# Weights of the sampling step laid out with four output rows side by side

## The reference

```python
samp = (v00 * (1 - wx) + v01 * wx) * (1 - wy) + (v10 * (1 - wx) + v11 * wx) * wy
return jnp.einsum('hwpc,hwp->hwc', samp, m)
```

## Time and profile before

| | |
|---|---|
| median of 3 runs | 6316.8 us (6306.65 to 6329.6) |
| profiled execution | 6298.82 us, span of the instructions 6297.0 us |
| VectorE (DVE) busy | 5355.5 us, 85% |
| TensorE (PE) busy | 3268.4 us, 52%, mean granted clock 0.763 |
| ScalarE (ACT) busy | 1498.1 us, 24% |
| GpSimd (POOL) busy | 529.3 us, 8% |
| DMA | 473.40 MB, 75 GB/s, 24.1% of 16 engines on SP's queue |

### The profile page before, as it was taken

One profiled execution on the slowest core, in us unless ns is written; L12 is line 12 of the kernel. 1 busy time (PEld: TensorE's weight loads), 2 busy tenths in 40 slices (PEclk: granted clock), 3 DMA queues, 4 the chain that ended last, 5 costly groups with the idle time before them and its releaser, 6 DMA issues.

```text
span 6297.0 us, 42119 instructions
## 1 busy us (share of the span) xinstructions
PE 3268.4 (52%) x15026; PEld 1887.4 (30%) x15026; DVE 5355.5 (85%) x6273; ACT 1498.1 (24%) x1409; POOL 529.3 (8%) x293
## 2 busy tenths in 40 slices
PE   4442645655455465645656455465645646455345
PEld 2211323332232233223333233233323333232233
DVE  5689898888989889898898989889898888989861
ACT  1312212222132223222222231223222222231210
POOL 0000101001010010001001010010001001010000
PEclk8676777878778687877878777687877878778677
DMA  7102122231222213122231222213122121222243
GB/s 322 50 17 64 56 73 68 60 95 40 77 87 61 77 53 102 41 75 68 60 95 50 76 78 67 71 53 102 41 75 75 57 91 50 70 83 62 70 110 87
DMA packets 511491, 473.40 MB, mean 75 GB/s; under 512 B 367984, under 2 KB 449904, under 8 KB 507568
## 3 DMA queue, kind: packets, MB, share of 16 engines
q1 hardware_dynamic: 507296, 463.25, 24.1%
q0 software_dynamic: 3984, 7.45, 0.5%
HBM read 229.00 MB, written 241.57 MB: 75 GB/s over the span
## 4 chain that ended last, share of the span: by engine, by line
DVE 68%; PE 16%; ACT 6%; issue 6%; POOL 3%; DMA 1%; SPq 1%; DVEq 0%; POOLq 0%; ACTq 0%
DVE spread L1102 9%; DVE partial L1092 9%; DVE spread L1092 6%; DVE qx L764 5%; DVE work L764 5%; PE ps L475 5%; DVE work L826 4%; DVE work L817 4%; DVE partial L1109 3%; PE ps L586 3%; PE ps L645 3%; DVE partial L1108 3%; DVE stats L735 2%; PE ps L656 2%; POOL small L1355 2%
## 5 line engine op out<-in xcount | busy, mean ns | idle before, releaser
L1102 DVE TENSOR_TENSOR spread<-spread,partial 128x1344 f32<-128x1344 f32 x384 | 685.4, 1785 | 13.3
L645 PE MATMUL ps<-band,near 128*16 128x128 f32 (+1 forms) x8192 | 655.3, 489 | 79.5 <-DMA near<-img_dram 79.5
L1092 DVE TENSOR_TENSOR partial<-haty,hatx 128x1344 f32<-128x1344 f32 x384 | 679.4, 1769 | 5.5
L543 PE MATMUL ps<-work,w2x 128*128 128x512 f32 x1152 | 558.0, 614 | 161.7 <-DVE work L817 150.7
L1224 ACT ACTIVATE xp<-x,small 128x1024 f32<-128x1024 f32 x128 | 280.2, 2332 | 1401.8 <-POOL small L1355 1401.8
L645 PEld LDWEIGHTS ps<-band,near 128*16 128x16 f32 x8192 | 486.5, 127 | 294.5 <-issue 103.4
L1092 DVE TENSOR_TENSOR spread<-haty,hatx 128x1344 f32<-128x1344 f32 x288 | 458.0, 1590 | 85.7 <-ACT qx L1261 64.4
L475 PE MATMUL ps<-qx,work 128*128 128x512 f32 x512 | 277.8, 704 | 333.4 <-DVE work L843 332.7
L656 PE MATMUL ps<-samp,wout 128*128 128x256 f32 x1024 | 296.7, 441 | 283.6 <-ACT samp L1330 260.8
L817 DVE SCALAR_TENSOR_TENSOR work<-ps,cols,qx 128x512 f32<-128x512 f32 x576 | 403.2, 746 | 14.3 <-PE ps L543 5.5
L586 PE MATMUL ps<-wts,work 128*128 128x432 f32 x512 | 223.0, 601 | 369.1 <-ACT work L1305 369.1
(11 more groups left out here) (229 smaller groups left out, 5262.5 us busy)
## 6 DMA issues: line engine op xcount, KB each, us to landing
band<-taps_dram SPq DMA_DIRECT2D x512, 288.0 KB
taps_dram<-partial SPq DMA_DIRECT2D x832, 72.0 KB, 2.1
near<-img_dram SPq DMA_DIRECT2D x256, 128.0 KB
img_dram<-band SPq DMA_DIRECT2D x6, 4096.0 KB, 40.9
om_now<-om SPq DMA_DIRECT2D x32, 576.0 KB, 5.2
om_dram<-om SPq DMA_DIRECT2D x32, 576.0 KB, 6.0
taps_dram<-partial SPq DMA_DIRECT2D x320, 54.0 KB, 2.1
x<-x_in SPq DMA_DIRECT2D x16, 1024.0 KB, 10.4
```

What stands on the lines that cost most here:

```text
L543: pe.matmul(bank(4 + i % 4), w2x[:, half, tap, :], tr[:, h * HALF:(h + 1) * HALF], start=True, stop=True).then_inc(s_w, 1)
L645: mm = pe.matmul(o, near[:, j, g * CG:(g + 1) * CG], band[:, :, a:z, j * G + g], start=False, stop=(j == JB - 1), skip_group_check=True)
L1092: return build(vec.tensor_tensor(o, haty[:, :, 3 * i:3 * i + 3, :].rearrange("p e j a -> p j e a"), cells, ALU.mult))
L1102: done = build(vec.tensor_tensor(skew, skew, spare, ALU.add))
```

## The change

Four output rows lie side by side in the band: its free axes become (block of four rows, column block, column slot, group, row in block). One block of four rows reaches 12 image rows, 96 partitions. The moving operand of a sampling matmul is then 2 blocks x 12 or 16 columns x 4 rows with the four rows adjacent in memory, 16 bytes. The matmuls keep their number and shapes.

What follows from it: the points of an image are put in another order, so that the partitions of a tile are 8 row blocks x 16 columns and the tile number holds the row in the block. The Gelu writes that order, in four instructions an image instead of two. A row of weights in the ring has 12 reached rows x 64 (zeros where a row doesn't reach), and lines 1108 and 1109 write it skewed, with a step of four numbers. SP writes a slot in eight DMAs instead of four. The band is loaded in 8 DMAs of 96 partitions. The copy to `samp` reads PSUM in the new order. Here `YB` is 8, `REACHED` 12, `QB` 2 and `YI` 4. The weights in DRAM are 26.7 MB instead of 18.9 MB (both are zeroed at the start), the rows that GpSimd gathers lie in the work tile, and the home pixel of a far tap takes one more instruction.

```diff
-        taps_dram = dram("taps_dram", [2, H, D * BW, SLOTS * HG])
+        taps_dram = dram("taps_dram", [2, YB, REACHED, ROW])
-        band = sb("band", [P, QROWS, SLOTS, HG])
+        band = sb("band", [P, QB, JB, SLOTS, G, YI])
-        gat = sb("gat", [P, 2, PAIR])
+        gat = work[:, 4 * N - 2 * PAIR:4 * N].rearrange("p (y c) -> p y c", y=2)
...
-                for yl in range(QROWS):
-                    sp.dma_start(band[yl * BW:yl * BW + D * BW, yl, :, :].rearrange("p s h -> p (s h)"),
-                                 taps_dram[n % 2, quarter * QROWS + yl]).then_inc(s_bl, 16)
+                for b in range(QB):
+                    for j in range(JB):
+                        source = taps_dram[n % 2, quarter * QB + b]
+                        cells = bass.AP(source.tensor, source.offset + j * BLOCK, [[ROW, REACHED], [CELL, BW], [1, CELL]])
+                        sp.dma_start(band[b * YI * BW:b * YI * BW + SPAN, b, j, :, :, :].rearrange("p s g i -> p (s g i)"), cells)\
+                            .then_inc(s_bl, 16)
...
-                    for a4 in range(TR):
...
-                        sp.dma_start(dst[:, :, at, slot, (first + move) * G:(last + move) * G],
-                                     src[:, :, first * G:last * G]).then_inc(s_w2[r], 16)
+                    first, last = max(0, -dx - half * XP), min(XP, W - dx - half * XP)
+                    seen = half * XP + first + dx
+                    for b in range(YB):
+                        to = taps_dram[n % 2, b]
+                        cells = bass.AP(to.tensor, to.offset + seen // BW * BLOCK + seen % BW * CELL + (seen % BW - dx + R) * RUN,
+                                        [[CELL + RUN, last - first], [ROW, REACHED], [1, RUN]])
+                        sp.dma_start(cells, ring[b * XP + first:b * XP + last, r, :].rearrange("p (r c) -> p r c", r=REACHED))\
+                            .then_inc(s_w2[r], 16)
...
-                                    .rearrange("p (y x) -> p y x", x=W)[:, :, j * BW - R + a:j * BW - R + z]
-                                mm = pe.matmul(o, near[:, j, g * CG:(g + 1) * CG], band[:, :, a:z, j * G + g],
+                                    .rearrange("p (b x i) -> p b x i", b=QB, i=YI)[:, :, j * BW - R + a:j * BW - R + z, :]
+                                mm = pe.matmul(o, near[:, j, g * CG:(g + 1) * CG], band[:, :, j, a:z, g, :],
...
-                    o = ring[:, r, :].rearrange("p (d a) -> p d a", d=D)
-                    wait(ve, s_w2[r], 16 * TR * (at // RING))
-                    ve.wait_ge(s_wb, build(vec.tensor_tensor(o, spread[:, 0, :, :], spread[:, 1, :, :], ALU.add)))
-                    vec.tensor_tensor(o, o, spread[:, 2, :, :], ALU.add).then_inc(s_wrow, 1)
+                    o = ring[:, r, :]
+                    o = bass.AP(o.tensor, o.offset, [list(o.ap[0]), [RUN, D], [RUN + 1, YI], [YI, G]])
+                    parts = [spread[:, j, :, :].rearrange("p d (i g) -> p d i g", i=YI) for j in range(3)]
+                    wait(ve, s_w2[r], 16 * YB * (at // RING))
+                    ve.wait_ge(s_wb, build(vec.tensor_tensor(o, parts[0], parts[1], ALU.add)))
+                    vec.tensor_tensor(o, o, parts[2], ALU.add).then_inc(s_wrow, 1)
...
-                    act.activation(acc[:, k, :].rearrange("p (x y) -> p y x", x=W), q[:, k, :].rearrange("p (y x) -> p y x", x=W),
-                                   ACT.Gelu, bias=col("ln_b", k), scale=col("ln_g", k)).then_inc(s_gelu, 1)
+                    for xb in range(XB):
+                        last = act.activation(acc[:, k, xb * HALF:(xb + 1) * HALF].rearrange("p (i b x) -> p b i x", i=YI, b=YB),
+                                              q[:, k, :].rearrange("p (b i c x) -> p b i c x", b=YB, i=YI, c=XB)[:, :, :, xb, :],
+                                              ACT.Gelu, bias=col("ln_b", k), scale=col("ln_g", k))
+                    last.then_inc(s_gelu, 1)
...
-                    act.activation(samp[:, :, :].rearrange("p g n -> p (g n)"), ps[:, 0:2, :].rearrange("p b n -> p (b n)"),
-                                   ACT.Copy).then_inc(s_samp, 1)
+                    act.activation(samp[:, :, :].rearrange("p g (b i x) -> p (g b) i x", b=QB, i=YI),
+                                   ps[:, 0:2, :].rearrange("p c (b x i) -> p (c b) i x", b=4, i=YI), ACT.Copy).then_inc(s_samp, 1)
```

More of the change, by code:

```diff
@@ L41 @@
 Q = QROWS * W
-SPAN = D * BW
-XROW = D * BW * SLOTS * HG
+XB, XP = 2, 16
+YI, YB = 4, 8
+QB = QROWS // YI
+REACHED = YI + 2 * R
+RUN = G * YI
+RUNS = REACHED * RUN
+SPAN = REACHED * BW
+CELL = SLOTS * RUN
+BLOCK = BW * (CELL + RUN)
+ROW = JB * BLOCK
 PAIR = C + CG
@@ L365, in _ @@
             sp.wait_ge(s_zero, 1)
-            blank = band[:, :, :, :].rearrange("p a b c -> p (a b c)")
-            width = QROWS * SLOTS * HG
+            blank = band[:, :, :, :, :, :].rearrange("p b j s g i -> p (b j s g i)")
+            width = QB * JB * CELL
             flat = img_dram.rearrange("s y x c -> (s y x c)").rearrange("(p n) -> p n", p=P)
@@ L423, in taps @@
                     sp.wait_ge(s_wrow, n * UNITS + u + 1)
-                    for a4 in range(TR):
[L425 to L430, removed]
-                        sp.dma_start(dst[:, :, at, slot, (first + move) * G:(last + move) * G],
-                                     src[:, :, first * G:last * G]).then_inc(s_w2[r], 16)
+                    first, last = max(0, -dx - half * XP), min(XP, W - dx - half * XP)
[6 more added lines that the diff above has]
+                            .then_inc(s_w2[r], 16)
                 yield FIRST_BAND_AT
                 for r in range(RING):
-                    sp.wait_ge(s_w2[r], 16 * TR * ROWS_A_SLOT * (n + 1))
+                    sp.wait_ge(s_w2[r], 16 * YB * ROWS_A_SLOT * (n + 1))
                 slot, uses = slot_of(n)
@@ L685, in _ @@
             vec = nc.vector
-            vec.memset(band[:, :, :, :], 0.0).then_inc(s_zero, 1)
+            vec.memset(band[:, :, :, :, :, :], 0.0).then_inc(s_zero, 1)
             vec.memset(xp[:, :, :, :], 0.0).then_inc(s_zero, 1)
@@ L692, in _ @@
             vec.memset(red[:, :], 0.0).then_inc(s_zero, 1)
+            vec.memset(ring, 0.0).then_inc(s_zero, 1)
+            ve.wait_ge(s_zero, 7)
             ve.wait_ge(s_load, 16 * N_LOAD)
@@ L922, in _ @@
             tap, cell, across, block, side_of = (floored[:, i:i + 1] for i in range(5))
-            group, tile, tap_xy, home = rs[:, 67:68], rs[:, 68:69], rs[:, 69:71], rs[:, 71:73]
+            group, tile, inside, tap_xy, home = rs[:, 67:68], rs[:, 68:69], rs[:, 176:177], rs[:, 69:71], rs[:, 71:73]
             table, pos, flr, spare2 = rs[:, 73:76], rs[:, 76:78], rs[:, 78:80], rs[:, 80:82]
@@ L978, in point_at @@
                 then(vec.scalar_tensor_tensor(out=block, in0=tap, scalar=-2.0, in1=block, op0=ALU.mult, op1=ALU.add))
-                then(vec.scalar_tensor_tensor(out=home[:, 0:1], in0=tile, scalar=float(BW), in1=side_of, op0=ALU.mult, op1=ALU.add))
-                then(vec.scalar_tensor_tensor(out=home[:, 0:1], in0=block, scalar=float(TR - JB * BW), in1=home[:, 0:1],
+                then(vec.scalar_tensor_tensor(out=home[:, 0:1], in0=block, scalar=float(XP), in1=point[:, 1:2], op0=ALU.mult, op1=ALU.add))
+                then(vec.scalar_tensor_tensor(out=home[:, 0:1], in0=side_of, scalar=-float(XP), in1=home[:, 0:1],
                                               op0=ALU.mult, op1=ALU.add))
-                then(vec.scalar_tensor_tensor(out=home[:, 1:2], in0=side_of, scalar=-float(H), in1=point[:, 1:2],
-                                              op0=ALU.mult, op1=ALU.add))
+                then(vec.scalar_tensor_tensor(out=inside, in0=block, scalar=-float(YI), in1=tile, op0=ALU.mult, op1=ALU.add))
+                then(vec.scalar_tensor_tensor(out=home[:, 1:2], in0=side_of, scalar=float(YI), in1=inside, op0=ALU.mult, op1=ALU.add))
                 then(vec.scalar_tensor_tensor(out=tap_xy[:, 1:2], in0=across, scalar=-3.0, in1=tap, op0=ALU.mult, op1=ALU.add))
```

16 lines of the change are left out of this document (8 added, 8 removed).

## The result

The changed kernel takes 6133.65 us in the median of four runs (6132.62 to 6137.16). The kernel before took 6321.15 on the same chip (6306.65 to 6329.6, four runs), so the ratio is 0.9707 with an interval of 0.9687 to 0.9726: 2.9% less, which is 185 us of the 6317 shown ahead (187.5 between these two medians). The forecast was 6275 us, 42 less than before. Its direction was right and its size was not: the time lies 141 us under the forecast, outside the forecast's own range (6170 to 6380) and inside the wide one (6090 to 6460), nearer to the rival of the free ring (6065), which did not happen.

The account below looks back on a forecast made before the run. VectorE was taken to bound the kernel, with 68% of the chain. 6297.0 - 280 + 210 + 28 = 6255 us of span, a median of about 6275; own range 6170 to 6380, wide range 6090 to 6460.

Parts of the forecast that it names:

- rival of the free ring: Lines 1108 and 1109 write as fast as before, so the gain stays whole: about 6065 us; chance 0.1.
- Burst length: Sampling matmuls, line 645: bursts fall from 10.2 to 6.7 us, saving 56 us in the images' first quarters.
- Stalls: VectorE instructions slowed during sampling bursts regain their pace: 200 us saved of at most 222, a tenth left in place.
- Gelu: Line 1305 becomes two halves writing runs of 16, 0.69 us each: 24 us saved, all on the path.
- Ring writes: Lines 1108 and 1109 write with a step of four words at 1.9 ns an element: 210 us added on the path.
- rival of the slow ring: Lines 1108 and 1109 at 2.45 ns an element cost 346 us instead of 210: about 6410 us, slower; chance 0.35.
- DMA issues and small ones: Weight-row issues at the end 5 us, last image's band loads 16, sample copy 4, far points' arithmetic 3: 28 us added.
- The copy of the samples: Reading PSUM with a step of four words adds 1 us if it doubles; 4 us on the path, last image only.
- the bursts stay as they are: Sampling bursts: four tiles together, not the step, hold VectorE up; 256 us not gained, about 6530 us; chance 0.08.

Follow-up runs that it names:

- before_groups_apart: The kernel before, with the four column tiles that run together given groups q, q+4, q+8, q+12, words 16 bytes apart instead of 4; 5949.90 us, ratio 0.9465.
- stepped_read: The changed kernel, but the sampling matmuls walk the band row by row, elements again 64 words apart; 6188.69 us, ratio 0.9832 to the kernel before.

## Why the prediction was right in sign and wrong in size

The step that failed is the one that names the cause, at the end of its first part: "the moving operand steps 64 words (256 bytes) from element to element, and four column tiles run together". It then let the step carry the gain and treated the four tiles as a reason for less gain. The runs show that what counts is four tiles together, all in the same 16 bytes of every 256; the step of 256 bytes keeps each of them there, and with the tiles apart the longest hold-up of a VectorE instruction in a burst is about 0.2 us (0.04 in before_groups_apart). The new layout ends this twice over: the four tiles stand 16 bytes apart, and their elements come in runs. The first alone removes the stalls (stepped_read); the runs shorten the bursts further. That the forecast had the sign right is in part luck: the end of the step, which it named as the cause, is worth 44 to 55 us on the path once the tiles are apart, against some 200 for the ring. The kernel is faster because the edit parts the tiles too.

The terms, by the prediction's own names:

- **Burst length.** Forecast 6.7 us, the middle between 3.2 and 10.2, and so 56 us on the path. Measured 3.3 to 4.1 in the middle of the run and 4.6 to 6.1 in the last image. Chain pieces of the sampling matmuls sum to 192 us before and 74 after, 118 less: twice the term, 62 us of the error. The 192 are 19 bursts and not the 16 of the forecast, since all four of the last image lie open. Taking the middle of two far bounds was the weak place. The experiments split it: 10.2 to 6.3 us by taking the tiles apart, 6.3 to 3.3 or more by the elements lying in runs of four. The lower bound, 0.9 ns a column as in the contiguous products of the earlier trace rows, was the right row to go by.
- **Stalls.** Forecast 200 of at most 222 us. before_groups_apart gains 338 us and changes nothing but this and the bursts; with 3.9 us less a burst on the path of 16 images and of the last image's three more, 19 x 3.9 = 74, the stalls come to 264 us. The error, 64 us, has two parts: a tenth, 22 us, was left in place and nothing of it stayed (line 1096: 4.359 us at most), and the forecast counted only the instructions marked in the earlier trace rows, while other VectorE and ScalarE instructions in the bursts were long too: ACT's pieces of the chain went from 383 to 321 us, of which Gelu explains 18. Line 1224 is the plainest case:

```profile
L1224 ACT ACTIVATE xp<-x,small 128x1024 f32<-128x1024 f32 x128 | 280.2, 2332 | 1401.8 <-POOL small L1355 1401.8
...
L1238 ACT ACTIVATE xp<-x,small 128x1024 f32<-128x1024 f32 x128 | 152.4, 1239 | 1338.4 <-POOL small L1372 1338.4
```

It is the same instruction, before and after: 2.33 us each for 1.24 (up to 6.4 before, 1.26 after, 1.28 in before_groups_apart).
- **Gelu.** Forecast 0.69 us a half, measured 0.80: 24 us became 2 x (2.15 - 1.60) x 16 = 18.
- **Ring writes.** The term without a row, and the one that came out best. Forecast 1.9 ns an element, measured (1.197 - 0.16) / 576 = 1.80; forecast 210 us on the path, measured 191 to 215. Two errors met in it: the price was somewhat too high (284 us of VectorE for 253), the share on the path too low (0.74 for 0.76 to 0.85). The rival of the slow ring (2.45 ns) and that of the free one (1.04) are both excluded.
- **DMA issues and small ones.** The bands' issues and landing in the last image grew, SP's pieces of the chain from 35 to 53 us and the DMAs' from 66 to 69: 21 us against 21 forecast. Within it landing grew less and issuing more. The copy of the samples did not double (1004 ns, 1011 before), which takes 4 us off.

By the measured terms: 118 + 264 + 18 gained, some 200 + 21 + 3 lost, 176 us net against 185 measured. The forecast had 280 - 238 = 42. Of the 143 us between, 126 lie in bursts and stalls. Both go one way, since the parted tiles stand behind all of the stalls and 74 of the bursts' 118 us.

The rival "the bursts stay as they are" held that the four tiles, not the step, keep VectorE waiting. Its mechanism was closer than the forecast's, and its time was wrong, because the changed layout moves the tiles apart as well, which neither the rival nor the forecast looked at. The diff had it in plain sight: `band[:, :, a:z, j * G + g]` becomes `band[:, :, j, a:z, g, :]`, so the next group stood 4 bytes away and now stands 16.

The prediction set the trace against the Trainium skill (SBUF — State Buffer, "Who interferes with whom"), by which TensorE keeps no engine waiting. The experiments bear the trace out: in the kernel before, those 264 us are gained by the order in which TensorE takes the groups. The rival of the slow ring drew on the Trainium skill's Vector Engine (DVE) Microarchitecture Reference, "Measured stream behaviour on trn2", where writes with small steps are the dearest (2.50 ns at 24 words); the trace has 1.80 ns at four words, so that order does not reach down to this step.

## What to carry to other kernels

When column tiles of TensorE run together, look at where each reads at the same moment: if all walk with a step of 256 bytes through the same 16 bytes of every 256, handing the tiles other groups (here two edited lines) may be worth more than a new layout. Where two causes go together in the kernel before, say which bytes each edit moves for both of them before crediting the gain to one. And weigh a layout by what each engine pays for it: here the runs of four save 44 to 55 us of TensorE on the path and cost VectorE some 200, and the layout comes out ahead only because it also parts the tiles; before_groups_apart has that part alone and is faster than the changed kernel by 153 us by the ratios and 184 by the medians.

## What the runs showed of the hardware that was not expected

**TensorE's reads can hold up VectorE, by address.** In the kernel before one VectorE product took 13.1 us instead of 4.35, and a sum took 3.94 for 1.56 while GpSimd was idle; with the tiles parted, and nothing else, the longest are 4.36 and 1.56.

**A walk in runs goes with the granted clock, a walk in steps does not.** Windows on four bursts of the changed kernel (length, busy us by engine in the order PE, PEld, DVE, ACT, POOL, granted clock, DMA share, GB/s):

```profile
3380.50:3384.00 3.50, 3.35 (x129) 3.03 (x128) 3.46 (x2) 1.38 (x2) 2.09 (x1) 1.00 0.02 5
5977.00:5982.50 5.50, 5.34 (x128) 4.59 (x128) 0.00 (x0) 0.03 (x1) 0.00 (x0) 0.60 0.17 55
6002.50:6007.20 4.70, 4.57 (x128) 3.97 (x128) 0.00 (x0) 0.02 (x1) 0.00 (x0) 0.70 0.20 60
6027.00:6033.00 6.00, 5.82 (x128) 4.79 (x120) 0.00 (x0) 0.10 (x1) 0.00 (x0) 0.53 0.14 46
```

and on three of stepped_read:

```profile
6029.60:6036.00 6.40, 6.28 (x128) 4.51 (x128) 0.00 (x0) 0.01 (x1) 0.00 (x0) 0.66 0.15 48
6055.40:6061.70 6.30, 6.24 (x128) 4.30 (x128) 0.00 (x0) 0.00 (x0) 0.00 (x0) 0.80 0.15 45
6081.80:6088.10 6.30, 6.25 (x128) 4.35 (x128) 0.00 (x0) 0.00 (x0) 0.00 (x0) 0.73 0.14 45
```

The clock column is 1.00 at 2.4 GHz and 0.50 at 1.2; the three bursts below 1.00 are those of the last image, before each of which TensorE waited for the band's DMAs. PE's busy time multiplied by that number is 3.3, 3.2, 3.2 and 3.1 us in the changed kernel. The burst at 3443.5, in the middle of the run, fits: 4.1 us at 0.79. In stepped_read a burst takes 6.2 to 6.3 us at 0.66, 0.73 and 0.80 alike, and also in the middle of the run, at 0.82 and 0.97. So in steps of 256 bytes something that the granted clock does not change sets the pace, 1.75 ns a column (6.28 us for 32 x 112), and in runs the clock does, 0.91 ns at full clock. In the last image, where the four bursts lie open, the runs are therefore worth only about 1 us a burst (21.4 us for 25.1 in all).

**ScalarE too pays for odd walks.** Gelu's half, written in runs of 16, takes 800 ns for 512 elements; written with a step of 32 words, 1024 took 2152 before. The contiguous line 1239 of the earlier trace rows has 687 ns, but it reads PSUM and is another function, so how much of the 113 ns between is the walk is not shown.
